# A state-space stage in 128 chunks: projections drained without a function table, one silu pass, x products first, output sums earlier, GpSimd by channel pairs

## What is computed

```python
xz = x @ in_proj_w.T
def run(xz_, A_log_):
    xi, z = jnp.split(xz_, 2, axis=-1)
    xi = silu(causal_dwconv1d(xi, conv1d_w, conv1d_b))        # 4 taps
    x_dbl = xi @ x_proj_w.T                                   # -> dt, Bm, Cm
    dt = softplus(x_dbl[..., :1] @ dt_proj_w.T + dt_proj_b)
    dA = exp(dt[..., None] * -exp(A_log_))                    # 18 channels x 16 states
    dBu = dt[..., None] * Bm[:, :, None, :] * xi[..., None]
    h = scan(h = dA * h + dBu)                                # along the sequence
    y = einsum('bldn,bln->bld', h, Cm) + xi * D
    return y * silu(z)
return (run(xz, A_log) + flip(run(flip(xz), A_b_log))) @ out_proj_w.T
```

## Time and profile before

| | us |
|---|---|
| median of 3 runs | 24739.93 |
| lowest and highest | 24702.33, 24742.21 |
| the profiled execution, device time | 24686.54 |
| its span | 24685.0 |
| VectorE busy | 15055.5 (61%) |
| ScalarE busy | 14220.0 (58%) |
| GpSimd busy | 9176.9 (37%) |

### The profile page before, as it was taken

How to read it: one execution, slowest core, us unless ns; L and a number is a source line. 1 busy time by engine, 2 the same in 40 slices (tenths; PEclk the granted TensorE clock), 3 DMA queues, 4 the chain that set the end, 5 groups by cost and what they waited for, 6 DMA issues and landing times. The chain is left out here.

```text
span 24685.0 us, 387087 instructions
## 1 busy us (share of the span) xinstructions
PE 20134.7 (82%) x135184; PEld 8113.1 (33%) x135184; DVE 15055.5 (61%) x15737; ACT 14220.0 (58%) x23206; POOL 9176.9 (37%) x7848
## 2 busy tenths in 40 slices
PE   6888888885548888888886999995458888888999
PEld 2333333332112222222223555552123333333444
DVE  8999999997147777777764666664143333333011
ACT  6899989885337777777755888784312222222111
POOL 6778878774027777777761000000000000000000
PEclk9999999997768888888887999897779999999999
DMA  1000000002930000000022211125921000011011
GB/s 64 12 12 12 12 12 11 12 12 79 160 96 17 17 18 17 17 17 17 18 54 41 37 34 34 36 34 127 206 87 24 23 23 23 23 29 31 31 41 44
DMA packets 1301493, 995.45 MB, mean 40 GB/s; under 512 B 748392, under 2 KB 1157584, under 8 KB 1265112
## 3 DMA queue, kind: packets, MB, share of 16 engines
q1 hardware_dynamic: 1199560, 849.64, 16.1%
q0 software_dynamic: 26624, 100.67, 1.5%
q10 hardware_dynamic: 74448, 33.14, 0.5%
HBM read 771.60 MB, written 211.63 MB: 40 GB/s over the span
## 5 line engine op out<-in xcount | busy, mean ns | idle before, releaser
L270 DVE TENSOR_TENSOR l_mx<-l_p_v,l_puN 128x2048 f32<-128x2048 f32 x2560 | 5637.1, 2282 | 153.1 <-PE l_p_s L485 140.1
L485 PE MATMUL l_p_s<-l_mx,l_w2z 128*32 128x512 f32 x32768 | 3835.9, 612 | 577.8 <-ACT l_mx L397 318.2
L290 POOL TENSOR_TENSOR l_mx<-l_pv,l_puP 128x2048 f32<-128x2048 f32 x1024 | 3715.3, 3644 | 326.1 <-PE l_p_s L485 320.3
L1196 POOL TENSOR_TENSOR l1m_hc<-l1m_hs,l1m_cs 128x512 f32<-128x512 f32 x2304 | 2921.4, 1268 | 7.6 <-DVE l1m_hs L1148 7.6
L2091 PE MATMUL l3a_p<-l3a_xn,l3a_w 128*128 128x512 f32 (+1 forms) x6144 | 2679.8, 599 | 274.6 <-ACT l3a_xn L1982 274.6
L1148 DVE TENSOR_TENSOR_SCAN l1m_hs<-l1m_da,l1m_carry,l1m_pu 128x512 f32<-128x512 f32 x2304 | 2824.3, 1267 | 106.1 <-ACT l1m_da L1066 2.2
L2197 POOL DMA_DIRECT2D l3b_xt<-x_after x64 | 33.9, 529 | 7651.0 <-DVE l3b_most L2326 5824.9
L1803 ACT ACTIVATE l1d_ab<-l1d_pt 128x1024 f32<-128x1024 f32 x2304 | 2297.4, 1024 | 672.5 <-PE l1d_pt L1557 659.2
L416 ACT ACTIVATE l_mx<-l_pv,l_puP 128x128 f32<-128x128 f32 x8192 | 2447.0, 394 | 0.8
L1138 DVE TENSOR_TENSOR l1m_pu<-l1m_pu,l1m_bs 128x512 f32<-128x512 f32 x2304 | 1476.2, 687 | 1095.4 <-PE l1m_pu L901 1095.4
L1681 DVE TENSOR_SCALAR l1d_hat<-l1d_ab 128x1024 f32<-128x1024 f32 x2304 | 1624.1, 705 | 799.4 <-ACT l1d_ab L1803 472.8
(11 more groups left out here) (301 smaller groups left out, 27695.3 us busy)
## 6 DMA issues: line engine op xcount, KB each, us to landing
n_xt<-x_after SPq DMA_DIRECT2D x48, 2048.0 KB
l3a_xb<-x_after SPq DMA_DIRECT2D x352, 256.0 KB, 4.1
l1o_img<-x_after SPq DMA_DIRECT2D x32, 2032.0 KB, 17.6
l_img<-x_after SPq DMA_DIRECT2D x32, 2032.0 KB, 17.1
l1m_sq<-seq SPq DMA_DIRECT2D x256, 144.0 KB
n_xt<-in_x_dram SPq DMA_DIRECT2D x16, 2048.0 KB
l_xs<-in_x_dram SPq DMA_DIRECT2D x128, 256.0 KB, 2.9
x_after<-l_ot SPq DMA_DIRECT2D x128, 256.0 KB, 2.4
```

The costliest lines, as they stand in the source:

```text
L270: v.tensor_tensor(mx[:, r % QB, :, :, :], columns.unsqueeze(1).broadcast_to([P, 4, G, P]), rows.broadcast_to([P, 4, G, P]), ALU.max).then_ ...
L290: g.tensor_tensor(mx[:, r % QB, :, :, :], pv[:, u, :, :].unsqueeze(1).broadcast_to([P, 4, G, P]), rows.broadcast_to([P, 4, G, P]), ALU.add ...
L485: ins = pe.matmul(p_s[R * q:R * (q + 1), 512 * u:512 * (u + 1)], w2z[:, 31 - r:63 - r], mx[:, r % QB, q, :, :].rearrange("p t v -> p (t v) ...
L1196: g.tensor_tensor(hc[:, (3 * u + p) % 6, part, :], hs[:, p % 3, part, :], cs[:, u, :], ALU.mult).then_inc(hc_done, 1)
```

## The change

The diff, cut to its core (the semaphore `silu_done` is new, and `use_of` numbers the uses of `pp`: X0, X1, Z0, Z1 now, X0, Z0, X1, Z1 before):

```diff
-        xi = m.sb("xi", [P, 2, 2, LC])
-        sz = m.sb("sz", [P, 2, 2, LC])
+        xz = m.sb("xz", [P, 2, 4, LC])
...
             def dt_proj(n, un, ho):
+                if ho == 0:
+                    pe.wait_ge(silu_done, n + 1)
...
                     if p == 1 and not last:
+                        x_proj(n, un, 1)
                         z_proj(n, un, 0)
                     if p == 2 and not last:
-                        x_proj(n, un, 1)
                         z_proj(n, un, 1)
+                    if p == 3:
+                        reduce(i, u, (0, 1))
                     if p == 5:
-                        reduce(i, u, (0, 1))
                         reduce(i, u, (2, 3))
                         reduce(i, u, (4,))
...
-                act.activation(xi[:, un, hf, :], pp[:, :], ACT.Silu, bias=cols[:, 0, hf:hf + 1]).then_inc(pp_drained, 1)
+                act.activation(xz[:, un, hf, :], pp[:, :], ACT.Identity, bias=cols[:, 0, hf:hf + 1]).then_inc(pp_drained, 1)
...
-                act.activation(sz[:, un, hf, :], pp[:, :], ACT.Silu).then_inc(pp_drained, 1)
+                act.activation(xz[:, un, 2 + hf, :], pp[:, :], ACT.Copy).then_inc(pp_drained, 1)
+
+            def gates(n, un):
+
+                act.wait_ge(pp_drained, use_of(n, Z1) + 1)
+                act.activation(xz[:, un], xz[:, un], ACT.Silu).then_inc(silu_done, 1)
...
                         if p == 0:
+                            a_of(n, un, jn)
                             gate_x(n, un, 0, True)
                         if p == 1:
+                            gate_x(n, un, 1, True)
                             gate_z(n, un, 0, True)
                         if p == 2:
-                            a_of(n, un, jn)
-                            gate_x(n, un, 1, True)
                             gate_z(n, un, 1, True)
+                            gates(n, un)
...
-                    if p == 2:
+                    if p == 1:
                         skip(i - 1, 1 - u, 1, i * D_IN + (8 + 4))
...
-                    g.tensor_tensor(carry[:, 1 - u, c:c + 1], hs[:, p % 3, part, LC - 1:], al[:, 1 - u, KEEP:], ALU.mult).then_inc(carry_ready, 1)
+                    g.tensor_tensor(carry[:, 1 - u, 2 * p:2 * p + 2], hs[:, p % 3, :, LC - 1],
+                                    al[:, 1 - u, KEEP:].broadcast_to([NB, 2]), ALU.mult).then_inc(carry_ready, 2)
...
-                g.tensor_tensor(hc[:, (3 * u + p) % 6, part, :], hs[:, p % 3, part, :], cs[:, u, :], ALU.mult).then_inc(hc_done, 1)
+                g.tensor_tensor(hc[:, (3 * u + p) % 6], hs[:, p % 3], cs[:, u:u + 1, :].broadcast_to([NB, 2, LC]),
+                                ALU.mult).then_inc(hc_done, 2)
...
+                    if not last and p == 8:
+                        steps(i + 1, 1 - u, 1)
+                    outputs(i, j, u, p, last)
+                    if p == 0:
+                        gated(i - 1, 1 - u, 1)
+                    if not last and p == 4:
+                        steps(i + 1, 1 - u, 0)
+                    if p == 8:
+                        g.wait_ge(pp_drained, (use_of(N, 0) if last else use_of(i + 1, OUT)) + 1)
+                        gated(i, u, 0)
```

More of the change, by code:

```diff
@@ L745, in state_space @@
     USES = 9
-    X0, Z0, X1, Z1, DT0, DT1, BB, CC, OUT = range(USES)
+    X0, X1, Z0, Z1, DT0, DT1, BB, CC, OUT = range(USES)
     LAST_OF = {0: 1, 1: 1, 2: 3, 3: 3, 4: 4, 5: 6, 6: 6, 7: 8, 8: 8}
@@ L787, in state_space @@
         (w_load, w_ready, a_exp, a_ready, pp_full, pp_drained, ab, e3, lg_ready, dt_ready, dtu_ready,
-         rates_done, inputs_done, exp_done, dbu_done, scan_done, carry_ready, hc_done, y_done, y1_done, y2_done) = (m.sem(n) for n in (
+         rates_done, inputs_done, exp_done, dbu_done, scan_done, carry_ready, hc_done, y_done, y1_done, y2_done, silu_done) = (m.sem(n) for n in (
              "w_load w_ready a_exp a_ready pp_full pp_drained ab e3 lg_ready dt_ready dtu_ready "
-             "rates_done inputs_done exp_done dbu_done scan_done carry_ready hc_done y_done y1_done y2_done").split())
+             "rates_done inputs_done exp_done dbu_done scan_done carry_ready hc_done y_done y1_done y2_done silu_done").split())
         s_in = [m.sem("s_in0"), m.sem("s_in1")]
@@ L1071, in _ @@
             gate_x(0, 0, 0, False)
+            gate_x(0, 0, 1, False)
             gate_z(0, 0, 0, False)
-            gate_x(0, 0, 1, False)
             gate_z(0, 0, 1, False)
+            gates(0, 0)
             softplus_parts(0, 0, False)
@@ L1154, in skip @@
                 dve.wait_ge(y2_done, i * 2 + (hf + 2))
-                dve.scalar_tensor_tensor(out=y1[:, hf, :], in0=xi[:, u, hf, :], scalar=cols[:, 2, hf:hf + 1],
+                dve.scalar_tensor_tensor(out=y1[:, hf, :], in0=xz[:, u, hf, :], scalar=cols[:, 2, hf:hf + 1],
                                          in1=py[:, :], op0=ALU.mult, op1=ALU.add).then_inc(y1_done, 1)
@@ L1200, in chunk @@
                 for p in range(PAIRS):
-                    for part in range(2):
-                        outputs(i, j, u, p, part, last)
-                        if (p, part) == (2, 0):
-                            gated(i - 1, 1 - u, 1)
-                        if (p, part) == (8, 1):
-                            g.wait_ge(pp_drained, (use_of(N, 0) if last else use_of(i + 1, OUT)) + 1)
-                            gated(i, u, 0)
-                        if not last and part == 1 and p in (5, 7):
-                            steps(i + 1, 1 - u, p // 7)
+                    if not last and p == 8:
+                        steps(i + 1, 1 - u, 1)
+                    outputs(i, j, u, p, last)
+                    if p == 0:
+                        gated(i - 1, 1 - u, 1)
[4 more added lines that the diff above has]
+                        gated(i, u, 0)
             over_chunks(g, chunk)
```

22 lines of the change are left out of this document (10 added, 12 removed).

## The result

The changed kernel takes 24377.2 us (median of four runs, 24351.4 to 24424.8) against 24741.1 us before (four runs, 24702.3 to 24776.3). The ratio is 0.9875, with a 95% interval of 0.985 to 0.990: 364 us or 1.5% faster. The prediction was 24470 us, in a range of 24230 to 24750. The profiled execution took 24396.4 us against 24686.5.

A forecast was written before the change was run, and what follows sets the result against it. The prediction took ScalarE's chain and TensorE's falling clock as the bound: 39.5 us a chunk at full clock plus 1.9 for the low clock makes 41.4, against 43.5, times 128 is 269 us less: 24470 us, range 24230 to 24750.

The forecast's parts named there:

- The chain: ScalarE's loads, drains and decays up to the second z product, then TensorE's blocks; VectorE idles 8.6 us a chunk.
- TensorE's new gaps: TensorE's idle times in the new order: 0.8 and 0.4 us, 1.5 for the silu pass, 0.6, then 2.6.
- Full-clock sum: Time of a chunk if TensorE's clock never falls: 39.8 us before the change, 39.5 after.
- Parts: ScalarE: four of eight loads go, 5.1 us a chunk, silu pass adds 1.9; GpSimd's pair product 2.45 with carry.
- The clock's share: Low clock after the change: 2.5 us in three chunks of four, 1.9 us a chunk on average, giving 41.4.
- pair 8's 1.2 us: Further lateness of VectorE's pair 8 from TensorE's low clock, after 0.8 us at pair 7.
- the prediction's own case of 24420 to 24610: The forecast case, 41.0 to 42.5 us a chunk, chance 0.46.
- the case of a high clock: Rival: TensorE's clock stays high, 39.5 us a chunk, 24228 us; chance 0.18.
- the fall behind step 6: TensorE's clock falls after its 2.6 us gap at t = 28.3 to 30.9, in about three chunks of four.
- longer than the 2.09 us: Ground for expecting a fall: TensorE's new 2.6 us gap exceeds the 2.09 us after which the clock fell before.
- The page's rule: Skill page's drain of about 1380 ns per ScalarE table switch; a further 5.5 us a chunk, 23766 us; no chance given.
- The slower rival: TensorE's clock also falls behind the silu wait: +3 on top of 1.9, 44.4 us a chunk, 24855 us; chance 0.15.

The follow-up runs named there:

- gap_filled_4: The changed kernel with four matmuls adding zeros in TensorE's gap ahead of the block of step 6; 24320.2 us, 39.43 us a chunk.
- silu_pass_alone: The kernel before with only the table-free drains and the one silu pass with its wait; 24352.0 us, 40.85 us a chunk.
- sums_back_at_5: The changed kernel with the sums of pairs 0 and 1 moved back from step 3 to step 5; 24338.0 us, 40.34 us a chunk.
- pass_longer: The changed kernel with one further copy of the 128x2048 tile on ScalarE ahead of the silu pass; 24583.8 us, 42.48 us a chunk.

## Why the prediction was right, point by point

*What bounds the kernel.* The chain was read rightly. TensorE's new gaps were, too: 0.8, 0.4, 1.5, 0.6 and 2.6 us were forecast, 0.78, 0.50, 1.56, 0.61 and 2.51 measured. VectorE's idle time stood ahead of the pairs named (3, 5 and 7), except that pair 8 did not wait.

*Full-clock sum.* 39.5 after and 39.8 before were forecast; 39.43 and 39.85 were measured with the gaps closed. (The terms written out add up to 39.57 and 39.77, so the two sums differ by 0.2.) The 39.85 is of a kernel whose sums had moved. Step by step the schedule can be followed in gap_filled_4, where the clock does not fall. Pair 0, the second x product and the block of step 6:

```profile
9021.25 1.27 DVE L1160 TENSOR_TENSOR l1m_pu<-l1m_pu,l1m_bs 128x512 f32<-128x512 f32 x2
```

```profile
9027.89 2.84 PE L861 MATMUL l1m_pp<-l1m_sq,l1m_wtap 96*128 96x512 f32 x6
...
9051.94 0.70 PE L903 MATMUL l1m_pu<-l1m_dts,l1m_sl 32*128 32x512 f32 x2 [0.66 <-ACT l1m_da L1085]
```

In t the two are at 6.6 and 30.7, where the prediction had 6.8 and 30.9. In the changed kernel itself they stand at t = 7.3 and 31.4, the silu pass at 16.3 (15.9 forecast), and VectorE's pair 7 at 33.5 where the sum had 32.1.

*Parts.* The loads went from eight to four (the row below against the x509 in the earlier trace rows), the silu pass took 1.910 us as the nearest row had it, the pair product 2.351 plus the carry as against 2.45 taken. GpSimd waited 5.32 us for the ln in front of pair 5, and it cost nothing:

```profile
L1073 ACT ACT_TABLE_LOAD x255 | 327.2, 1283 | 6.4 <-PE l1m_pr L895 1.8
```

```profile
9036.95 1.26 POOL L1185 TENSOR_TENSOR l1m_dts<-l1m_rl,l1m_lg 128x512 f32<-128x512 f32 x1 [5.32 <-ACT l1m_lg L1050]
```

*The clock's share was mis-sized.* I took 1.9 us a chunk from a low stretch of 6.9 us in three chunks of four. Measured is 40.99 - 39.43 = 1.56: a stretch of 3.4 us in every chunk, over the block and a part of the C product. It shows in two places: from the block of step 6 to VectorE's pair 7 are 2.12 us (9039.60 to 9041.72) in place of 1.17, which is 0.95, and the second x product of the next chunk starts 0.66 us later than at the full clock (t = 7.30 against 6.64). Together that is 1.6. Of pair 8's 1.2 us nothing came: it follows pair 7 by 3.76 us, without a wait. I had taken the shortest stretch seen before as the shortest there is, and the same mistake made my expectation for silu_pass_alone wrong by 2 us a chunk. The forecast of 41.4 us a chunk against 40.99 measured accounts for 52 of the 93 us by which 24470 was too high. The other 41 are not in the stage: it gained 321 us, the medians 364, and 291 when both kernels were run again. Where they are is not traced; the profiled executions differ by 290, and `deform` took 36 us more in the one of after. The 24377 us also lie below the prediction's own case of 24420 to 24610, between it and the case of a high clock. So the direction and the fall behind step 6 were foreseen, while the size of its cost was partly luck: 2.5 us in three chunks of four had been taken, 1.56 in every chunk came, and the two errors work against each other.

*Where the old clock fell* was read from one chunk of four. The prediction named the gaps of 1.54 and 2.09 us ahead of the fall. In 94 of 126 chunks the clock had fallen already at the second x product, with only 1.54 and 0.68 us idle before it, as in the row of 8995.86 in the earlier trace rows. So "longer than the 2.09 us" was no bound to go by, though a fall behind 2.51 us did come, in every chunk and not in three of four.

*The page's rule.* ScalarE goes from the load at 9023.28 (1.28 us) to the pass at 9024.57 without a gap, and from the pass to the next load at 9026.50. The drain of about 1380 ns that the Trainium skill adds to each switch ("ScalarE: Activation LUTs", section "What ACT_TABLE_LOAD costs") does not appear here either.

*The slower rival* asked for a fall behind the silu wait. In silu_pass_alone and sums_back_at_5 the clock does fall there (gaps of 2.99 and 2.55 us), and neither is slow. Where the clock falls both there and behind step 6, in the second chunk shown of pass_longer, the two cost 2.6 us; the rival had put 1.9 + 3. In the changed kernel, whose wait for the pass is 1.56 us, it happened in none of the 126 chunks.
